# Attention masks as two products of 64 rows, and rope of k and square sums over both halves at once, in a six-layer windowed attention kernel

## The chip, the cores and the metric

The kernel runs on one core of a Trainium2 chip. The metric is device time in microseconds (us) of one execution. Five engines work side by side and meet through semaphores: TensorE (PE, matrix products and transposes; its weight loads are PEld), VectorE (DVE), ScalarE (ACT), GpSimd (POOL) and SyncE (SP, which issues the DMAs). SBUF is the working memory of 128 partitions, PSUM has 8 banks of 512 float32 a partition, into which TensorE writes.

## The reference, cut to what matters

The input `x` is (8, 512, 128). It is normalized, and the output is `x` plus a causal attention with relative positions plus a stack of six layers. Only the six layers matter here. Each has an attention over windows of 32 positions with 16 heads of 64, and then a gated feed-forward part:

```python
def attn_layer(x, Wqkv, qs, ksc, Wo):          # WINDOW = 32, HEADS = 16, DIM_HEAD = 64
    q, k, v = jnp.split(x @ Wqkv, 3, -1)       # each (b, n, 1024), then per head
    q = l2norm(q) * qs
    k = l2norm(k) * ksc
    q = q * cos * scale + rotate_half(q) * sin * scale
    k = k * cos * inv + rotate_half(k) * sin * inv
    out = local_attention(q, k, v)
    return out.reshape(b, n, INNER) @ Wo

def local_attention(q, k, v):                  # bk2, bv2: the window before and the own one
    mask = (it < jb) | (it > jb + w) | (jb == -1)
    sim = jnp.einsum('bhwie,bhwje->bhwij', bq, bk2) * QK_SCALE
    sim = jnp.where(mask, -jnp.finfo(sim.dtype).max, sim)
    attn = jax.nn.softmax(sim, -1)
    return jnp.einsum('bhwij,bhwje->bhwie', attn, bv2)

for i in range(DEPTH):                         # DEPTH = 6
    x = attn_layer(shift_tokens(x), Wqkv[i], q_scale[i], k_scale[i], Wo[i]) + x
    x = ffn_layer(shift_tokens(x), ln_g[i], ln_b[i], W1[i], b1[i], W2[i], b2[i]) + x
```

## The kernel before, in words

A first stage of about 570 us (`relative_attention`) computes the relative attention. Then `windowed_layers` runs the six layers, five in a hardware loop and the last written out. The order of work on every engine is written out by hand; semaphores with counts hold the engines together.

**Slots.** The attention of a layer goes over 8 sequences of 4 tiles with 128 positions each. A slot works on up to three tiles at a time: the new one ("age 0": project, square, rope), the one before ("age 1": turn q and k, masks, scores), and the one before that ("age 2": softmax, values, output product). `slot(lay, s, t, ages)` on each engine writes one slot. Of the 33 slots of a layer 32 have age 1, and 30 have both ages 0 and 2.

**TensorE in a slot** (L1370 to L1414): project v half 0 (bank 7), k halves 0 and 1 (banks 4 and 5) and q half 0 (bank 6), three products each of 128 by 512; turn the weights of half 0 (`turn_weights`, waits for `e_made` and `pw_made`); project q half 1 (bank 7); turn the weights of half 1; `mix_half(0)`, 64 small products of 64 rows by 32 columns; `turn_q(0)` and `turn_q(1)`, eight transposes into banks 4 and 5, which must wait until the rope of k has read those banks; `mix_half(1)`; project v half 1 into bank 6, which waits for the rope of q half 0; `turn_k(0)`, `turn_mixed(0)`, `turn_mixed(1)`, `turn_k(1)`; the masks; `score_half(0)`, 64 small products; the output product, 16 products (L1410); `score_half(1)`, which releases `s_mm`. The wait of `turn_q` is

```python
if project_new:
    pe.wait_ge(rk_made, at(T, 0, 2, c + 1))
```

**Masks** (L1402 to L1405): scores are made in banks 2 and 3, even heads (`par` 0) and odd heads (`par` 1). Before the scores each bank is filled with the mask, as a product of the identity (bfloat16, 128 by 128) with the mask of 128 rows, repeated for 8 heads to 512 columns; the scores are added onto it.

**VectorE in a slot** (L1776 to L1829): row maxima over both banks (L1782, waits for `s_mm`); two subtractions (L1788), each releasing `e_made`; rope of k half 0, half 1, rope of q half 0 (`rope_half`, three operations each: L1740 with 512 elements, L1741 and L1742 with 256); for each half of the mixed values a reciprocal and a product (`on`, L1810 and L1812); rope of q half 1; `lengths`: two sums of squares (L1747, 1024 elements each), then `square_root`, a chain of small operations that begins with L1755; at last the sum into `state` (L1826).

**ScalarE in a slot** does, in this order: copy v half 0, square k half 0 (L1562), exponentials half 0 (L1587, waits for `e_made`), square k half 1, exponentials half 1, copy turned weights half 0, square q half 0, and so on. `square` releases `sqk_made` or `sqq_made` by 1 per half, and waits for `ss_made` of the tile before.

**GpSimd in a slot** carries a part of kT (L1210), adds the two parts of the rope for k and for q (L1176, 1024 elements), refines the inverse square roots (L139 to L145) and scales q and k (L1181); in every second slot it splits half of the next input (L1057).

The `opening` of a layer, during the feed-forward part of the layer before, makes the first tile with `rope_half` and `lengths` in another order.

Of the kernel before, what the change touches and what calls it, by code (L numbers as in the profile page):

```python
# [25 lines left out]
X = mybir.AxisListType.X  # L26
# [26 lines left out]
C_FART = C_FAR + P  # L53
C_NEAR = C_FART + P
C_PART = C_NEAR + H
# [5 lines left out]
def constants():  # L61
# [20 lines left out]
    c[:, C_MQ:C_MQ + 2 * W] = shut  # L82
    first = (np.arange(P)[:, None] < W) & (k2 < W)
    c[:, C_MQ0:C_MQ0 + 2 * W] = np.where(first, MASKED, shut)
    far = np.where(np.arange(P)[None, :] >= np.arange(P)[:, None], MASKED, 0.0)
    c[:, C_FAR:C_FAR + P] = far
    c[:, C_FART:C_FART + P] = far.T
    c[0, C_NEAR:C_NEAR + H] = MASKED
# [12 lines left out]
def bc(ap, where, n):  # L101

    ap = ap.unsqueeze(where)
    return ap.broadcast_to([n if i == where else m for i, m in enumerate(ap.shape)])
# [768 lines left out]
def windowed_layers(nc, Wqkv, qs, ks, Wout, ln_g, ln_b, W1, b1, W2, b2, state, total, rank, out):  # L873
# [8 lines left out]
    with ExitStack() as ctx:  # L882
# [50 lines left out]
        ident = rank["const"][:, C_ID:C_ID + P]  # L933
        id_bf, mask_bf, mean_w = rank["id_bf"], rank["mask_bf"], rank["mean_w"]
        mask_q = {t: mask_bf[:, 2 * W * (t == 0):2 * W * (t == 0) + 2 * W] for t in range(TPS)}
# [73 lines left out]
        def at(T, back, n, i):  # L1009


            return n * (T - back + CREDIT) + i
# [234 lines left out]
        def _(pe):  # L1247
# [45 lines left out]
            def slot(lay, s, t, ages):  # L1293
# [106 lines left out]
                if score:  # L1400
                    turn_k(1)
                    pe.wait_ge(on_made, at(T, 2, 2, 2))  # L1402
                    for par in range(2):
                        pe.matmul(PS[:, 2 + par, :], id_bf[:], bc(mask_q[tile1], 1, PAIRS),
                                  start=True, stop=False, skip_group_check=True)  # L1405
                    score_half(0)
# [298 lines left out]
        def _(dve):  # L1705
# [25 lines left out]

            def rope_half(T, t, i, c, bank, squared, turned, added, done):
                dve.wait_ge(squared, at(T, 0, 2, c + 1))
                dve.wait_ge(turned, at(T, 2, 2, 2))
                dve.wait_ge(added, at(T, 1, 1, 1))
                src = PS[:, bank, :].rearrange("p (h d) -> p h d", h=8)
                cols = slice(512 * c, 512 * (c + 1))
                o1 = t1[:, t % 2, i, cols].rearrange("p (h d) -> p h d", h=8)
                o2 = t2[:, i, cols].rearrange("p (h d) -> p h d", h=8)
                dve.tensor_tensor(o1, src, bc(rope[:, 2 * i, t, :], 1, 8), ALU.mult)  # L1740
                dve.tensor_tensor(o2[:, :, 0:32], src[:, :, 32:64], bc(rope[:, 2 * i + 1, t, 0:32], 1, 8), ALU.mult)  # L1741
                dve.tensor_tensor(o2[:, :, 32:64], src[:, :, 0:32], bc(rope[:, 2 * i + 1, t, 32:64], 1, 8),  # L1742
                                  ALU.mult).then_inc(done, 1)

            def square_sum(T, i, squared):
                dve.wait_ge(squared, at(T, 0, 2, 2))
                dve.tensor_reduce(ss[:, H * i:H * (i + 1)], sq[:, i, :].rearrange("p (h d) -> p h d", h=H),  # L1747
                                  X, ALU.add).then_inc(ss_made, 1)

# [20 lines left out]
            def lengths(T):  # L1770
                square_sum(T, 0, sqq_made)
                square_sum(T, 1, sqk_made)
                square_root(T)

            def slot(lay, s, t, ages):
# [21 lines left out]
                if 0 in ages:  # L1797
                    rope_half(T, t, 1, 0, 4, sqk_made, kt_mm, addk_made, rk_made)
                    rope_half(T, t, 1, 1, 5, sqk_made, kt_mm, addk_made, rk_made)
                    rope_half(T, t, 0, 0, 6, sqq_made, qt_mm, addq_made, rq_made)  # L1800
# [150 lines left out]
```

## Time and profile before

| | us |
|---|---|
| median of 3 runs | 3954.24 (3954.11 to 3961.58) |
| the profiled execution, its own time | 3959.98 |
| its span in the profile | 3958.2 |
| TensorE busy | 3716.9 (94%) |
| VectorE busy | 3286.9 (83%) |
| GpSimd busy | 2598.7 (66%) |
| ScalarE busy | 2178.6 (55%) |

The span is the time from the first to the last instruction in the trace. Times of rows are measured from its start. An engine counts as busy while an instruction runs; TensorE's products overlap, and their ends are modelled, so the distance from one start to the next says more of their cost than their length. Idle time is put down to what ended it; "issue" is idle time in which no semaphore was waited for.

### The profile page before, as it was taken

Reading aid. Unit: us, or ns where it says so; the run is one execution under the profiler, and the core shown is the slowest. Engines: PE = TensorE matmul, PEld = TensorE weight load, DVE = VectorE, ACT = ScalarE, POOL = GpSimd, SP = SyncE. Lnnn points to the kernel's source line nnn. Section 1 sums busy time; section 2 is a strip of 40 time slices with the busy share of each in tenths; the row PEclk is TensorE's granted clock in tenths of the full one; section 3 lists DMA queues with packets and bytes.
Section 4 is the critical chain, followed back from the end, with each engine's and each line's share of the span. In section 5 each row is a group of like instructions: output and inputs, shape, how many; then the busy total and the mean of one; then the engine's idle time right before and its main releaser. Section 6 shows DMA issues by size and latency. Waiting matters only on the chain.

```text
span 3958.2 us, 165481 instructions
## 1 busy us (share of the span) xinstructions
PE 3716.9 (94%) x67712; PEld 2864.8 (72%) x67712; DVE 3286.9 (83%) x6981; ACT 2178.6 (55%) x3886; POOL 2598.7 (66%) x3029
## 2 busy tenths in 40 slices
PE   6999979999999999999999999999999999999998
PEld 3555547878767787677787677787677776777776
DVE  7666659999789899788998798997889897888886
ACT  3555545666546666456665465665466564565552
POOL 4555538887457777368787287874577773687770
PEclk8999989999999999999999999999999999999999
DMA  1000012222212222122222122222122221222220
GB/s 43 4 6 4 6 34 66 57 56 59 58 34 58 60 60 58 35 53 56 60 60 52 33 65 60 56 57 56 35 57 60 60 56 37 53 55 59 60 52 22
DMA packets 136325, 189.11 MB, mean 48 GB/s; under 512 B 38006, under 2 KB 58484, under 8 KB 135412
## 3 DMA queue, kind: packets, MB, share of 16 engines
q1 hardware_dynamic: 135540, 178.17, 17.6%
q8 instruction: 551, 9.03, 1.0%
q14 instruction: 234, 1.92, 0.2%
HBM read 22.61 MB, written 2.10 MB: 6 GB/s over the span
## 4 chain that ended last, share of the span: by engine, by line
POOL 39%; PE 22%; issue 20%; DVE 2%; POOLq 2%; ACT 0%; DMA 0%; SPq 0%; DVEq 0%; ACTq 0%
POOL t L1176 18%; POOL t L1181 8%; PE PS L1264 3%; PE PS L1250 3%; POOL xl L1057 3%; PE PS L1469 2%; PE PS L1252 2%; PE PS L1251 2%; POOL rn L145 2%; PE PS L1410 2%; POOL rn_tmp L141 2%; POOL rn_tmp L143 2%; POOL rn_tmp L139 2%; PE PS L1288 2%; PE PS L1274 1%
## 5 line engine op out<-in xcount | busy, mean ns | idle before, releaser
L1176 POOL TENSOR_TENSOR t<-t 128x1024 f32<-128x1024 f32 x384 | 908.3, 2373 | 263.3 <-DVE t L1742 263.3
L1535 ACT ACTIVATE va<-PS 128x512 f32<-128x512 f32 x384 | 230.1, 599 | 956.3 <-PE PS L1252 956.3
L1181 POOL TENSOR_TENSOR t<-t,rn 128x1024 f32<-128x1024 f32 x384 | 724.1, 1907 | 28.4 <-POOL rn L145 25.9
L1740 DVE TENSOR_TENSOR t<-PS,rope 128x512 f32<-128x512 f32 x768 | 521.7, 679 | 23.6 <-ACT sq L1562 18.1
L1250 PE MATMUL PS<-w_hi,xh 128*128 128x512 f32 x1152 | 514.8, 447 | 25.7 <-DVE xl L1057 10.1
L1562 ACT ACTIVATE sq<-PS 128x512 f32<-128x512 f32 x768 | 455.7, 594 | 38.3 <-PE PS L1252 22.3
L1252 PE MATMUL PS<-w_lo,xh 128*128 128x512 f32 x1152 | 460.8, 400 | 0.0
L1251 PE MATMUL PS<-w_hi,xl 128*128 128x512 f32 x1152 | 458.9, 398 | 0.0
L1264 PE MATMUL PS<-constants,t 128*128 128x128 f32 x3072 | 444.7, 278 | 9.5 <-POOL t L1181 7.6
L1747 DVE TENSOR_REDUCE ss<-sq 128x16 f32<-128x1024 f32 x384 | 448.0, 1207 | 0.0
L1264 PEld LDWEIGHTS PS<-constants,t 128*128 128x128 f32 x3072 | 352.8, 142 | 58.2 <-POOL t L1181 9.9
L1410 PE MATMUL PS<-oT,w_out 128*128 128x128 f32 x3072 | 393.3, 281 | 0.0
L1288 PE MATMUL PS<-vs,shared 64*32 64x65 f32 x18432 | 337.2, 225 | 45.3 <-issue 45.3
L1410 PEld LDWEIGHTS PS<-oT,w_out 128*128 128x128 f32 x3072 | 357.8, 191 | 17.7
L1274 PEld LDWEIGHTS PS<-kT,qT 64*32 64x32 f32 x24576 | 273.9, 105 | 127.3 <-issue 103.3
L1274 PE MATMUL PS<-kT,qT 64*32 64x64 f32 x24576 | 342.7, 225 | 15.0 <-POOL kT L1210 7.8
L1288 PE MATMUL PS<-va,shared 64*32 64x65 f32 x6144 | 338.9, 225 | 14.6 <-issue 14.6
L1288 PEld LDWEIGHTS PS<-vs,shared 64*32 64x32 f32 x18432 | 265.0, 105 | 111.0 <-issue 110.8
L1741 DVE TENSOR_TENSOR t<-PS,rope 128x256 f32<-128x256 f32 x768 | 316.3, 412 | 0.0
L1742 DVE TENSOR_TENSOR t<-PS,rope 128x256 f32<-128x256 f32 x768 | 315.8, 411 | 0.0
L1782 DVE TENSOR_REDUCE m<-PS 128x16 f32<-128x1024 f32 x192 | 234.9, 1224 | 87.4 <-PE PS L1274 85.2
L1250 PEld LDWEIGHTS PS<-w_hi,xh 128*128 128x128 f32 x1152 | 218.3, 190 | 95.7 <-issue 30.0
(172 smaller groups left out, 8112.8 us busy)
## 6 DMA issues: line engine op xcount, KB each, us to landing
vs<-va SPq DMA_DIRECT2D x768, 130.0 KB
vs<-va SPq DMA_DIRECT2D x768, 65.0 KB
t<-in_L_ffn_Wqkv SPq DMA_DIRECT2D x18, 512.0 KB, 4.4
w_out<-in_L_ffn_Wo SPq DMA_DIRECT2D x6, 512.0 KB, 3.9
a_normed<-in_L_attn_x SPq DMA_DIRECT2D x8, 256.0 KB, 6.4
a_xo<-in_L_attn_x SPq DMA_DIRECT2D x8, 256.0 KB, 2.9
out<-total SPq DMA_DIRECT2D x8, 256.0 KB, 3.5
w_raw<-in_L_ffn_W SPq DMA_DIRECT2D x6, 341.0 KB
```

Source lines behind the costliest of these rows:

```text
L1176: pool.tensor_tensor(mine[:, i, :], mine[:, i, :], t2[:, i, :], ALU.add).then_inc(done, 1)
L1181: pool.tensor_tensor(h, h, bc(rn[:, H * i:H * (i + 1)], 2, HB), ALU.mult).then_inc(done, 1)
L1250: pe.matmul(out, hi, w_hi, start=True, stop=False)
L1251: pe.matmul(out, lo, w_hi, start=False, stop=False)
L1252: return pe.matmul(out, hi, w_lo, start=False, stop=True)
L1264: last = pe.transpose(PS[:, bank, P * j:P * (j + 1)], source(j), ident)
L1274: last = pe.matmul(PS[W * w:W * (w + 1), 2 + par, 2 * W * pair:2 * W * (pair + 1)], qT[rows, pair, W * w:W * (w + 1)], kT[rows, t % 2, pai ...
L1288: last = pe.matmul(PS[W * w:W * (w + 1), (0, 2)[c] + par, HB1 * (pair % 4):HB1 * (pair % 4 + 1)], pT[rows, pair, W * w:W * (w + 1)], v, st ...
L1410: last = pe.matmul(PS[:, y_at, 0:P], w_out[:, pair, :], oT[:, pair, :], start=(pair == 0), stop=(pair == PAIRS - 1))
L1562: act.activation(sq[:, i, 512 * c:512 * (c + 1)], PS[:, bank, :], ACT.Square).then_inc(done, 1)
L1740: dve.tensor_tensor(o1, src, bc(rope[:, 2 * i, t, :], 1, 8), ALU.mult)
L1747: dve.tensor_reduce(ss[:, H * i:H * (i + 1)], sq[:, i, :].rearrange("p (h d) -> p h d", h=H), X, ALU.add).then_inc(ss_made, 1)
```

## The change

Three edits. The masks are no longer made with the identity and 128 rows. A new constant table of 128 columns (`C_SEL`, two copies over 64 rows each) picks for each of the 128 queries its row among 64, so that rows 0 to 63 of the mask are enough for bank 2 and rows 64 to 127 for bank 3. The table comes as bfloat16 with the masks, as part of `mask_bf`. The rope of k is one call over 16 heads in place of two calls over 8; it waits for both squares, reads banks 4 and 5 together, and releases `rk_made` by 2 at its end. The two square sums are one operation over 2048 elements, which releases `ss_made` by 2. The rope of q and the openings keep the halves.

```diff
+C_SEL = C_FART + P
+C_NEAR = C_SEL + P
...
-    first = (np.arange(P)[:, None] < W) & (k2 < W)
+    first = (np.arange(P)[:, None] % (2 * W) < W) & (k2 < W)
...
+    row, query = np.arange(P)[:, None] % (2 * W), np.arange(P)[None, :]
+    c[:, C_SEL:C_SEL + P] = np.where(query < W, query == row, query % W + W == row)
...
-        id_bf, mask_bf, mean_w = rank["id_bf"], rank["mask_bf"], rank["mean_w"]
+        mask_bf, mean_w = rank["mask_bf"], rank["mean_w"]
+        sel_bf = mask_bf[:, C_SEL - C_MQ:C_SEL - C_MQ + P]
...
                     for par in range(2):
-                        pe.matmul(PS[:, 2 + par, :], id_bf[:], bc(mask_q[tile1], 1, PAIRS),
+                        rows = slice(HB * par, HB * (par + 1))
+                        pe.matmul(PS[:, 2 + par, :], sel_bf[rows, :], bc(mask_q[tile1][rows, :], 1, PAIRS),
                                   start=True, stop=False, skip_group_check=True)
...
-            def rope_half(T, t, i, c, bank, squared, turned, added, done):
-                dve.wait_ge(squared, at(T, 0, 2, c + 1))
+            def rope_heads(T, t, i, heads, src, squared, turned, added, done):
+                n = heads.stop - heads.start
+                dve.wait_ge(squared, at(T, 0, 2, heads.stop // 8))
                 dve.wait_ge(turned, at(T, 2, 2, 2))
                 dve.wait_ge(added, at(T, 1, 1, 1))
-                src = PS[:, bank, :].rearrange("p (h d) -> p h d", h=8)
-                cols = slice(512 * c, 512 * (c + 1))
-                o1 = t1[:, t % 2, i, cols].rearrange("p (h d) -> p h d", h=8)
-                o2 = t2[:, i, cols].rearrange("p (h d) -> p h d", h=8)
-                dve.tensor_tensor(o1, src, bc(rope[:, 2 * i, t, :], 1, 8), ALU.mult)
-                dve.tensor_tensor(o2[:, :, 0:32], src[:, :, 32:64], bc(rope[:, 2 * i + 1, t, 0:32], 1, 8), ALU.mult)
-                dve.tensor_tensor(o2[:, :, 32:64], src[:, :, 0:32], bc(rope[:, 2 * i + 1, t, 32:64], 1, 8),
-                                  ALU.mult).then_inc(done, 1)
...
-            def square_sum(T, i, squared):
-                dve.wait_ge(squared, at(T, 0, 2, 2))
-                dve.tensor_reduce(ss[:, H * i:H * (i + 1)], sq[:, i, :].rearrange("p (h d) -> p h d", h=H),
-                                  X, ALU.add).then_inc(ss_made, 1)
+                src = src.rearrange("p (h d) -> p h d", h=n)
+                o1 = t1[:, t % 2, i, :].rearrange("p (h d) -> p h d", h=H)[:, heads, :]
+                o2 = t2[:, i, :].rearrange("p (h d) -> p h d", h=H)[:, heads, :]
+                dve.tensor_tensor(o1, src, bc(rope[:, 2 * i, t, :], 1, n), ALU.mult)
+                dve.tensor_tensor(o2[:, :, 0:32], src[:, :, 32:64], bc(rope[:, 2 * i + 1, t, 0:32], 1, n), ALU.mult)
+                dve.tensor_tensor(o2[:, :, 32:64], src[:, :, 0:32], bc(rope[:, 2 * i + 1, t, 32:64], 1, n),
+                                  ALU.mult).then_inc(done, n // 8)
+
+            def rope_half(T, t, i, c, bank, squared, turned, added, done):
+                rope_heads(T, t, i, slice(8 * c, 8 * (c + 1)), PS[:, bank, :], squared, turned, added, done)
...
             def lengths(T):
-                square_sum(T, 0, sqq_made)
-                square_sum(T, 1, sqk_made)
+                dve.wait_ge(sqq_made, at(T, 0, 2, 2))
+                dve.wait_ge(sqk_made, at(T, 0, 2, 2))
+                dve.tensor_reduce(ss[:], sq[:].rearrange("p i (h d) -> p (i h) d", h=H), X, ALU.add).then_inc(ss_made, 2)
                 square_root(T)
...
-                    rope_half(T, t, 1, 0, 4, sqk_made, kt_mm, addk_made, rk_made)
-                    rope_half(T, t, 1, 1, 5, sqk_made, kt_mm, addk_made, rk_made)
+                    rope_heads(T, t, 1, slice(0, H), PS[:, 4:6, :].rearrange("p b n -> p (b n)"),
+                               sqk_made, kt_mm, addk_made, rk_made)
                     rope_half(T, t, 0, 0, 6, sqq_made, qt_mm, addq_made, rq_made)
```

## Rows read from the trace of the kernel before

Columns of a timeline: start in us from the start of the span, length in us, engine, line, operation, output<-inputs, array form (rows*columns for TensorE), shape, type, count merged; in brackets the idle time before and what ended it.

**Rows 1.** Busy time by engine in 500 us inside the layers; clock, DMA.

```profile
2000.00:2500.00 500.00, 476.60 (x9395) 378.10 (x9374) 431.77 (x934) 281.29 (x522) 341.57 (x408) 0.99 0.21 53
```

**Rows 2.** Waits: who waited for whom, us in total, times, longest.

```profile
PEld PS L1274 <- issue: 103.3, 229, 3.1
...
DVE m L1782 <- PE PS L1274: 85.2, 156, 1.2
...
PE PS L1288 <- issue: 59.9, 76, 1.5
```

**Rows 3.** Timeline of TensorE in one slot: start, length, line.

```profile
2020.13 1.09 PE L1264 MATMUL PS<-constants,t 128*128 128x128 f32 x8
...
2021.94 0.50 PE L1250 MATMUL PS<-w_hi,xh 128*128 128x512 f32 x1
...
2024.49 0.59 PE L1404 MATMUL PS<-mask_bf,id_bf 128*128 128x512 bf16 x2
```

**Rows 4.** Timeline of VectorE in the same slot.

```profile
2017.24 0.68 DVE L1740 TENSOR_TENSOR t<-PS,rope 128x512 f32<-128x512 f32 x1
2017.84 0.41 DVE L1741 TENSOR_TENSOR t<-PS,rope 128x256 f32<-128x256 f32 x1
2018.17 0.41 DVE L1742 TENSOR_TENSOR t<-PS,rope 128x256 f32<-128x256 f32 x1
...
2019.43 0.41 DVE L1742 TENSOR_TENSOR t<-PS,rope 128x256 f32<-128x256 f32 x1
2019.76 0.68 DVE L1740 TENSOR_TENSOR t<-PS,rope 128x512 f32<-128x512 f32 x1
...
2023.83 0.41 DVE L1742 TENSOR_TENSOR t<-PS,rope 128x256 f32<-128x256 f32 x1
2024.16 2.33 DVE L1747 TENSOR_REDUCE ss<-sq 128x16 f32<-128x1024 f32 x2
...
2028.68 1.23 DVE L1782 TENSOR_REDUCE m<-PS 128x16 f32<-128x1024 f32 x1 [0.41 <-PE PS L1274]
```

**Rows 5.** Timeline of ScalarE, this slot and the one before.

```profile
2003.34 0.58 ACT L1562 ACTIVATE sq<-PS 128x512 f32<-128x512 f32 x1
...
2016.87 0.62 ACT L1587 ACTIVATE shared<-shared 128x512 f32<-128x512 f32 x1
2017.39 0.59 ACT L1562 ACTIVATE sq<-PS 128x512 f32<-128x512 f32 x1
```

**Rows 6.** Timeline of TensorE, turn of q in the slot before.

```profile
2006.07 1.09 PE L1264 MATMUL PS<-constants,t 128*128 128x128 f32 x8
```

**Rows 7.** Timeline of GpSimd's adds and of VectorE's L1755.

```profile
2008.56 4.70 POOL L1176 TENSOR_TENSOR t<-t 128x1024 f32<-128x1024 f32 x2
...
2024.32 2.37 POOL L1176 TENSOR_TENSOR t<-t 128x1024 f32<-128x1024 f32 x1 [0.56 <-DVE t L1742]
...
2012.47 0.84 DVE L1755 TENSOR_SCALAR ss<-ss 128x32 f32<-128x32 f32 x1
```

**Rows 8.** Timeline of TensorE in narrow windows, at changes of form.

```profile
2010.33 0.27 PE L1264 MATMUL PS<-constants,t 128*128 128x128 f32 x1
2010.43 0.59 PE L1404 MATMUL PS<-mask_bf,id_bf 128*128 128x512 bf16 x2
...
2010.65 0.38 PE L1404 MATMUL PS<-mask_bf,id_bf 128*128 128x512 bf16 x1
2010.96 0.27 PE L1274 MATMUL PS<-kT,qT 64*32 64x64 f32 x6
...
2005.07 0.27 PE L1264 MATMUL PS<-constants,shared 128*128 128x128 f32 x1
2005.28 0.24 PE L1288 MATMUL PS<-vs,shared 64*32 64x65 f32 x1
```

**Rows 9.** Groups by line: busy, mean ns, idle before.

```profile
L1274 PE MATMUL PS<-kT,qT 64*32 64x64 f32 x24576 | 342.7, 225 | 15.0 <-POOL kT L1210 7.8 <-issue 5.7
```

**Rows 10.** Timeline of GpSimd at the start of the run.

```profile
16.75 0.61 POOL L381 COPY state<-a_xT 128x513 f32<-128x513 f32 x1 [4.08 <-ACT a_xT L660]
```

More of the change, by code:

```diff
@@ L53 @@
 C_FART = C_FAR + P
-C_NEAR = C_FART + P
+C_SEL = C_FART + P
+C_NEAR = C_SEL + P
 C_PART = C_NEAR + H
```

## Prediction

> **What bounds the kernel.** I read the busy times by stretches first. In 500 us of the windowed layers TensorE is busy 476.6 us and VectorE 431.8, at a granted clock of 0.99 [rows 1]. So the clock is at its upper level (2.4 GHz) and two engines are near full. To decide between them I read one slot of the layers on each engine's timeline. The masks of one tile start at 2010.43 and of the next at 2024.49, so a slot takes 14.06 us [rows 3, 8]. In it TensorE goes from one group to the next with no wait for another engine that is worth naming: turn of q, second half of the mixed values, projection, turns, masks, scores, output product, scores. VectorE is done earlier: before it takes the row maxima it sits idle 0.41 us for the last score [rows 4], and over the run that wait comes 156 times, 85.2 us in all [rows 2]. Hence a delay of TensorE shows in full in the time, and VectorE has about half a microsecond of room in a slot. There is one more loss on TensorE: 59.9 us in 76 pauses "for issue" inside the products of weights and values, where no semaphore is waited for [rows 2]. A delay just ahead of such a pause may be swallowed by it.
>
> **Part 1, the rope of k over both halves.** It replaces six operations by three. Spacing on VectorE is 0.60 us for 512 elements a partition (2017.24 to 2017.84) and 0.33 for 256 (2017.84 to 2018.17) [rows 4], that is about 0.06 fixed and 0.27 for 256 elements. With 1024, 512 and 512 elements the three take 1.14 + 0.60 + 0.60 = 2.34 in place of 6 operations with 2.52 (2017.24 to 2019.76). The work shrinks by 0.18 us a slot.
>
> But the new first operation needs the squares of *both* halves, since it waits for sqk at heads.stop // 8 = 2, where the first half of the old form waited for 1. ScalarE makes them in its own order: square of half 0, exponentials of half 0 (which wait for VectorE's subtraction), square of half 1. In this slot the exponentials start at 2016.87 and the second square runs 2017.39 to 2017.98 [rows 5]. VectorE comes free at 2017.24. It must now wait until about 2018.03 (0.05 for the handover; the nearest row is 0.08 from VectorE's end at 2024.24 to GpSimd's start at 2024.32 [rows 4, 7]). All that is queued behind on VectorE starts later: the rope of q, reciprocals, on, the square sums.
>
> Who waits for it: the rope's result is now released once, at its end. 2018.03 + 1.14 + 0.60 + 0.68 (the last 512 end to end) = 2020.45, against 2019.84 for the second half now. TensorE's turn of q writes banks 4 and 5, from which the rope reads, and waits for this; it starts at 2020.13 now [rows 3]. With 0.05 of handover it starts at 2020.50, a stall of 0.35 to 0.37. The slot before says the same: second square ends 2003.92 [rows 5], plus 0.05 + 2.42 + 0.05 = 2006.44, and the turn of q started at 2006.07 [rows 6]: 0.37. I take 0.35, a little lower because the handovers may be 0.03. The bounds: 0.25, if the longer operations have a smaller fixed part than I take, and 0.45.
>
> What comes after has room. The rope of q's first half would end at 2018.03 + 2.34 + 0.60 + 0.33 + 0.41 = 2021.71; the projection that waits for it starts at 2021.94 now and at 2022.29 after the stall [rows 3]. The second result of on trails TensorE's own products, so it moves by the same 0.35 and no more. So the stall is paid once per slot. It comes in slots that have both a new tile and weights to turn: 30 in each of 6 layers, 180. Gross 180 x 0.35 = 63 us.
>
> How much of it falls into the pauses for issue? They stand right behind the turn of q, in the second half of the mixed values. 76 pauses of 0.79 us mean [rows 2] could take at most 76 x 0.35 = 27 us. I take 22, since some are shorter than the stall. Net +41 us; bounds +18 (0.25 x 180 = 45, less 27) and +81 (0.45, none swallowed).
>
> **Part 2, square sums at once.** The two reductions take 2.33 us [rows 4] and become one; by the fixed part that saves 0.06. I cost it at nothing, because the next operation, the maximum with 1e-24 in L1755, doesn't start freely. In the slot where GpSimd's two adds run from 2008.56 for 4.70 us, to 2013.26, this small operation begins at 2012.47 and lasts 0.84, to 2013.31 [rows 7]. It ends with the add. In the other slot the add of q starts 0.08 behind the rope and takes 2.37 [rows 7], as long as the reductions. Saving at most 192 x 0.06 = 12 us of VectorE time, it is covered by GpSimd's add and then by VectorE's 0.41 of idle time; the bound is 0 to 2 us of gain, for slots without that idle time.
>
> **Part 3, masks on 64 rows each.** Per slot two products of 128 rows and 512 columns become two of 64 rows in different halves of the array and different banks. Do such halves run together? The score products (64 rows by 32 columns, alternating halves) take 342.7 us for 24576, 14 ns each though one lasts 225 [rows 9]; so many run at once, in both halves. So the second mask should start next to the first, saving the 0.22 between 2010.43 and 2010.65 [rows 8]. What speaks against it is the change of form. From the last turn to the first mask, both 128 by 128, it is 0.10 (2010.33 to 2010.43), but from the last turn to products of 64 by 32 it is 0.21 (2005.07 to 2005.28) [rows 8]. And from the second mask to the scores it is 0.31 (2010.65 to 2010.96), 0.09 more than mask to mask. Each change of form costs 0.09 to 0.11. Now there is one between turns and scores; then there are two, 128x128 to 64x128 to 64x32. From last turn to first score: now 0.10 + 0.22 + 0.31 = 0.63; after 0.21 + 0.01 + 0.31 = 0.53. Gain 0.10 to 0.12 by rounding; 0.11 x 192 tiles = 21 us. Bounds: 0.22 x 192 = 42 if the step to 64x128 is free, and a loss of 0.11 x 192 = 21 if the halves run one behind the other.
>
> The Trainium skill has both sides: TensorE: Matmul & The Clock Gate (Part 3, measured speedup) has tiles in different row groups start about 4 ns apart, with no price for the change, which makes 42; TensorEngine Tiling (Array Packing), Key Properties, says that changing the mode drains the array, which makes 21. Rows 8 agree with the second.
>
> Not all of it is kept. The loads of the score products wait for issue 103.3 us in 229 pauses, nearly all hidden behind products [rows 2], but the second half of the scores, after the output product, is sometimes held up by them; with masks that end earlier such pauses grow. I take a third away: gain 14 us.
>
> The new table of 128 columns makes one load and one cast at the start longer. GpSimd, which casts, is idle 4.08 us right after that work until ScalarE releases it [rows 10], and the cast is well under that: nothing.
>
> **The sum.** 41 - 14 - 0 = +27 us. The profiled execution took 3959.98 with a span of 3958.2; its layers' slots are those of every run. Against the median of 3954.2 this gives 3981. A change under 0.2%, 8 us, can't be told from none here.
>
> **Rivals.**
> 1. *The change of form is free* (chance 0.12). Gain 42 less a third = 28; 3954 + 41 - 28 = 3967. For: the halves surely run together in the scores. Against: [rows 8].
> 2. *Issue swallows the stall in all slots* (0.13), the case on the other side. TensorE would be paced by how its instructions arrive, and a pause lets them get ahead, so that later pauses vanish too: 59.9 us of them [rows 2] would pay for the 63. Then 3954 + 3 - 21 = 3936. It becomes "faster" only where less than 13 of the 63 us are left beside the full 21 of the masks. Against: the pauses stand in 76 of 192 slots, and the slot shown runs without any. The Trainium skill (Runtime: NRT & Kernel Launch, Instruction fetch mechanics) has instructions arrive in blocks of 256; no row here shows a block's arrival.
> 3. *Nothing is swallowed* (0.12): 3954 + 63 - 14 = 4003, if the pauses only move behind the stall.
> 4. *Halves one behind the other* (0.05): 3954 + 41 + 21 = 4016, or a little less where pauses hide part.
> 5. *The change does nothing that shows* (0.10): VectorE's wait of 0.8 us is there, but stall and masks cancel, the stall nearer to 0.25. 45 - 27 = 18, less 14 to 21: 3954, from 3946 to 3962.
> My forecast has 0.48.
>
> **Numbers.** 3981, range 3950 to 4004: it leaves out rival 2, rival 4 and an edge of rival 5, together 0.2. The forecast's own range is 3970 to 3998. Faster: rival 2, 0.13. Same: rival 5 and the low edge of rival 1, 0.12. Slower 0.75.
>
> **What the profile after would show.** The first rope operation with 1024 elements with an idle of 0.7 to 0.9 us before it, released by ScalarE's square, about 180 times. The turn of q idle before it 0.35, released by VectorE's rope. Masks with 64 rows, a few ns apart, 0.2 behind the last turn. Pauses for issue in the mixed values smaller by about 20 us. The idle before the row maxima still above 0.2. I am wrong if the turn of q doesn't wait, if the pauses shrink by much more than 27 us, or if the two masks lie 0.2 apart.

## The result and the profile after

The changed kernel takes 3996.03 us in the median of 4 runs (3992.15 to 3999.37), the kernel before beside it 3954.3 us: a ratio of 1.0095, 95% interval 1.0076 to 1.0115. That is 42 us slower by the medians, 38 by the ratio. The forecast was +27, that is 3981, with a range of 3950 to 4004. The profiled execution of the changed kernel has a span of 3997.3 us, 39 more than before.

The waits of the changed kernel (who waited for whom, us in total, times, longest):

```profile
DVE t L1749 <- ACT sq L1569: 153.4, 192, 3.2
...
DVE m L1790 <- PE PS L1280: 94.0, 174, 1.1
...
PE PS L1270 <- DVE t L1751: 76.2, 182, 2.0
...
PE PS L1294 <- issue: 33.7, 69, 1.1
```

Two waits have grown from little. VectorE's first rope operation (now L1749) waits for ScalarE's square 153.4 us in 192 places, where the kernel before has 18.1 us in 14. TensorE's transposes (now L1270) wait for VectorE's rope 76.2 us in 182 places, where it has 1.3 us. One line shrank: the pauses for issue in the mixed values, 59.9 us before, are 33.7. VectorE's idle time before the row maxima, 94.0 us in all, is larger than the 85.2 of [rows 2], so VectorE isn't what holds the next slot back.

One slot of the changed kernel, first ScalarE, then VectorE, then TensorE (timeline: start, length, engine, line, ..., idle time before):

```profile
2022.10 0.63 ACT L1594 ACTIVATE shared<-shared 128x512 f32<-128x512 f32 x1
2022.63 0.58 ACT L1569 ACTIVATE sq<-PS 128x512 f32<-128x512 f32 x1
```

```profile
2023.24 1.23 DVE L1749 TENSOR_TENSOR t<-PS,rope 128x1024 f32<-128x1024 f32 x1 [0.81 <-ACT sq L1569]
2024.39 0.68 DVE L1750 TENSOR_TENSOR t<-PS,rope 128x512 f32<-128x512 f32 x1
2024.98 0.68 DVE L1751 TENSOR_TENSOR t<-PS,rope 128x512 f32<-128x512 f32 x1
2025.58 0.68 DVE L1749 TENSOR_TENSOR t<-PS,rope 128x512 f32<-128x512 f32 x1
```

```profile
2025.81 1.06 PE L1270 MATMUL PS<-constants,t 128*128 128x128 f32 x8 [0.38 <-DVE t L1751]
```

It reads like [rows 4] and [rows 5] with the wait put in. On ScalarE the exponentials of half 0 come first, and the second square ends at 2023.21. The rope starts 0.03 later, after 0.81 us idle. Its three operations take 1.15, 0.59 and 0.68 us, the first two counted to the next start. TensorE turns q 0.15 us after the last of them ends (2025.66).

The masks, in a narrow window of TensorE's timeline, and where the scores begin:

```profile
2015.18 0.27 PE L1270 MATMUL PS<-constants,t 128*128 128x128 f32 x1
2015.38 0.39 PE L1411 MATMUL PS<-mask_bf 64*128 64x512 bf16 x2
...
2015.70 0.28 PE L1280 MATMUL PS<-kT,qT 64*32 64x64 f32 x7
```

Both masks lie within 0.39 us, one mask's length, and start 3 ns apart in the median (in [rows 8] two took 0.59). The first starts 0.20 behind the last turn, where it was 0.10, and the scores start 0.32 behind the masks. From last turn to first score it is 0.52 in place of 0.63: a gain of 0.11, as the sum had it.

### The profile page after: what moved, and what is told of

Read it like the earlier page. It is cut to its first block, busy times and chain, and to the rows that moved or that the text cites. A ratio compares the mean times of both kernels' runs of the same rounds, so it can differ in the third digit from the quotient of the medians.

```text
span 3997.3 us, 164737 instructions
## 1 busy us (share of the span) xinstructions
PE 3708.9 (93%) x67712; PEld 2857.6 (71%) x67712; DVE 3235.6 (81%) x6231; ACT 2176.8 (54%) x3886; POOL 2597.8 (65%) x3029
## 4 chain that ended last, share of the span: by engine, by line
POOL 31%; PE 26%; issue 19%; DVE 5%; ACT 2%; POOLq 1%; DMA 0%; DVEq 0%; SPq 0%; ACTq 0%
POOL t L1182 15%; POOL t L1187 6%; PE PS L1270 5%; PE PS L1417 3%; PE PS L1280 3%; PE PS L1256 3%; PE PS L1476 3%; PE PS L1258 2%; PE PS L1257 2%; POOL xl L1063 2%; POOL rn L150 2%; POOL rn_tmp L146 2%; POOL rn_tmp L148 2%; PE PS L1294 2%; POOL rn_tmp L144 2%
## 5 line engine op out<-in xcount | busy, mean ns | idle before, releaser
L1749 DVE TENSOR_TENSOR t<-PS,rope 128x512 f32<-128x512 f32 (+1 forms) x582 | 496.8, 854 | 158.3 <-ACT sq L1569 153.4
L1270 PE MATMUL PS<-constants,t 128*128 128x128 f32 x3072 | 440.1, 277 | 81.7 <-DVE t L1751 76.2
L1270 PEld LDWEIGHTS PS<-constants,t 128*128 128x128 f32 x3072 | 355.2, 142 | 135.1 <-issue 103.0
L1780 DVE TENSOR_REDUCE ss<-sq 128x32 f32<-128x2048 f32 x192 | 436.4, 2273 | 0.0
L1417 PEld LDWEIGHTS PS<-oT,w_out 128*128 128x128 f32 x3072 | 358.0, 191 | 18.1 <-issue 0.3
L1542 ACT ACTIVATE qT<-PS 128x512 f32<-128x512 f32 x384 | 208.8, 595 | 149.4 <-PE PS L1270 149.2
L1750 DVE TENSOR_TENSOR t<-PS,rope 128x256 f32<-128x256 f32 (+1 forms) x582 | 289.8, 498 | 0.0
L1751 DVE TENSOR_TENSOR t<-PS,rope 128x256 f32<-128x256 f32 (+1 forms) x582 | 289.4, 497 | 0.0
```

Of the source, the lines that this page charges most:

```text
L1270: last = pe.transpose(PS[:, bank, P * j:P * (j + 1)], source(j), ident)
L1417: last = pe.matmul(PS[:, y_at, 0:P], w_out[:, pair, :], oT[:, pair, :], start=(pair == 0), stop=(pair == PAIRS - 1))
L1542: copy = lambda o, i: act.activation(o, i, ACT.Copy)
L1749: dve.tensor_tensor(o1, src, bc(rope[:, 2 * i, t, :], 1, n), ALU.mult)
```

## The experiments

Each experiment was timed beside the kernel before, in four groups. That kernel's own median was 3962.7, 3964.4, 3965.9 and 3978.7 us in them, against 3954.3 beside the changed kernel, so the ratios are what is compared.

### Each part alone

**masks_only**, the changed kernel with the rope of k and the square sums as before:

```diff
-                    rope_heads(T, t, 1, slice(0, H), PS[:, 4:6, :].rearrange("p b n -> p (b n)"),
-                               sqk_made, kt_mm, addk_made, rk_made)
+                    rope_half(T, t, 1, 0, 4, sqk_made, kt_mm, addk_made, rk_made)
+                    rope_half(T, t, 1, 1, 5, sqk_made, kt_mm, addk_made, rk_made)
...
-                dve.tensor_reduce(ss[:], sq[:].rearrange("p i (h d) -> p (i h) d", h=H), X, ALU.add).then_inc(ss_made, 2)
+                for i, squared in enumerate((sqq_made, sqk_made)):
+                    dve.wait_ge(squared, at(T, 0, 2, 2))
+                    dve.tensor_reduce(ss[:, H * i:H * (i + 1)], sq[:, i, :].rearrange("p (h d) -> p h d", h=H),
+                                      X, ALU.add).then_inc(ss_made, 1)
```

> The kernel before with the masks on 64 rows alone (rope of k and square sums as before). My theory: from the last turn to the first score TensorE needs 0.11 us less in each of 192 tiles, 21 us, of which issue pauses in the second half of the scores take back a few: 3954 - 17 = 3937, ratio 0.995 to 0.997, with no waits of the turn of q for VectorE's rope. Rival, the extra change of form costs more than the pairing gains and the masks are part of the loss: 3960 or more. Rival, the change of form only shows in these few starts and the gain is the full 0.21: 3918 to 3925.

Measured: ratio 0.996 (0.9944 to 0.9975), 16 us faster. The masks are the good part, of the size of the sum's net term (14). TensorE's transposes wait for the rope only 3.1 us, in 6 places.

**rope_only**, the kernel before with only `rope_heads` and its call for k (the call is shown):

```diff
-                    rope_half(T, t, 1, 0, 4, sqk_made, kt_mm, addk_made, rk_made)
-                    rope_half(T, t, 1, 1, 5, sqk_made, kt_mm, addk_made, rk_made)
+                    rope_heads(T, t, 1, slice(0, H), PS[:, 4:6, :].rearrange("p b n -> p (b n)"),
+                               sqk_made, kt_mm, addk_made, rk_made)
```

> The kernel before with the rope of k over both halves alone. My theory: the whole loss is here. The turn of q waits 0.40 to 0.45 us for VectorE in 180 slots, 72 to 80 us, of which 25 to 30 fall into pauses for issue: 3954 + 50 = 4004, range 3998 to 4012, ratio 1.011 to 1.015, more than the full change. Rival, the loss comes from another part (the single square sum, the masks): this one stays within 3950 to 3975. Rival, the loss of the full change needs both, because the masks' saved time makes the stall longer: 3975 to 3990.

Measured: ratio 1.0104 (1.0085 to 1.0124), 41 us slower. Its waits:

```profile
DVE t L1742 <- ACT sq L1562: 152.8, 192, 4.5
...
PE PS L1264 <- DVE t L1744: 76.0, 182, 2.0
...
PE PS L1288 <- issue: 36.3, 72, 1.1
```

These are the three lines of the changed kernel again, within 3 us, without the masks. So the loss is here, and the stall doesn't depend on the masks. The time came 9 us below the 50 that I expected.

**sums_only**, the kernel before with the single square sum of the change:

```diff
-                square_sum(T, 0, sqq_made)
-                square_sum(T, 1, sqk_made)
+                dve.wait_ge(sqq_made, at(T, 0, 2, 2))
+                dve.wait_ge(sqk_made, at(T, 0, 2, 2))
+                dve.tensor_reduce(ss[:], sq[:].rearrange("p i (h d) -> p (i h) d", h=H), X, ALU.add).then_inc(ss_made, 2)
```

> The kernel before with the two square sums as one operation. My theory: 0.06 us less of VectorE work per slot, hidden by GpSimd's add that the next small operation waits for and by VectorE's idle time before the row maxima: 3952 to 3956, ratio 0.999 to 1.001. Rival, VectorE is on the path in many slots: 192 x 0.06 = 12 us faster, 3942. Rival, the later release of the first half's sum holds up ScalarE's square of the next k: slower by more than 4 us.

Measured: ratio 1.0005 (0.9993 to 1.0018), no difference. Where the saved 0.06 us went shows in the operation behind the sum:

```profile
L1755 DVE TENSOR_SCALAR ss<-ss 128x32 f32<-128x32 f32 x192 | 84.4, 440 | 6.6
```

It lasts 440 ns in the mean; before, its 192 took 75.2 us, 392 ns each, so 9 of the 12 us are lost again here. In 182 of the 192 places it starts while GpSimd's add runs, and there it always ends 0.03 to 0.04 us after the add does (worked out from the trace).

**masks_sums**, the changed kernel with only the rope of k back in halves (the first part of the diff of masks_only).

> The changed kernel with the rope of k back in two halves: masks on 64 rows and one square sum. My theory: the two good parts without the bad one, 3934 to 3940, ratio 0.995 to 0.997, the same as the masks alone within 3 us. Rival, the parts interact (the shorter masks bring VectorE onto the path, so that the shorter sum now counts): 3925 to 3932, clearly below the masks alone.

Measured: ratio 0.9977 (0.9957 to 0.9997), just above the range expected. It isn't told apart from the masks alone; there is no sign that the shorter sum counts.

### What in the rope costs: the wait or the width

**first_in_halves**, the changed kernel, but the first rope operation of k in two halves, each behind its own square:

```diff
-                dve.wait_ge(squared, at(T, 0, 2, heads.stop // 8))
+                if n < H:
+                    dve.wait_ge(squared, at(T, 0, 2, heads.stop // 8))
...
-                dve.tensor_tensor(o1, src, bc(rope[:, 2 * i, t, :], 1, n), ALU.mult)
+                if n == H:
+                    for c in range(2):
+                        part = slice(8 * c, 8 * (c + 1))
+                        dve.wait_ge(squared, at(T, 0, 2, c + 1))
+                        dve.tensor_tensor(o1[:, part, :], src[:, part, :], bc(rope[:, 2 * i, t, :], 1, 8), ALU.mult)
+                else:
+                    dve.tensor_tensor(o1, src, bc(rope[:, 2 * i, t, :], 1, n), ALU.mult)
```

> The changed kernel, but the first of the three rope operations of k is made in two halves, each waiting for its own square; the other two stay over both halves. My theory: the cost is the wait for ScalarE's second square ahead of the first operation, not the width. VectorE then works through half 0 while the second square is made, the rope ends 0.5 us earlier, 0.1 ahead of the turn of q, and the stall of 0.44 is gone: ratio to before 0.995 to 0.998, as masks_sums. Rival, the single release of both halves at the end is what costs: the turn of q still waits more than 0.2 us in most slots, ratio 1.004 or more.

Measured: ratio 0.9963 (0.9949 to 0.9977). VectorE in one slot, and TensorE's wait for the rope over the whole run:

```profile
2000.36 0.68 DVE L1754 TENSOR_TENSOR t<-PS,rope 128x512 f32<-128x512 f32 x1
2001.25 0.69 DVE L1754 TENSOR_TENSOR t<-PS,rope 128x512 f32<-128x512 f32 x1 [0.21 <-ACT sq L1569]
2001.86 0.68 DVE L1757 TENSOR_TENSOR t<-PS,rope 128x512 f32<-128x512 f32 x1
2002.46 0.68 DVE L1758 TENSOR_TENSOR t<-PS,rope 128x512 f32<-128x512 f32 x1
```

```profile
PE PS L1270 <- DVE t L1758: 5.8, 4, 1.8
```

Half 0 is worked on while the second square is made. In the slot shown 0.21 us of idle time are left, where the slot of the changed kernel had 0.81, and the turn of q waits in 4 places in place of 182. The release is still single and two operations still span both halves. So the cost is the wait ahead of the first operation. This version is faster than both kernels (15 us under the kernel before), as masks_only is, and has four rope operations for k in place of six. Against six (masks_sums, 0.9977) the gain of having four isn't told from none.

**after_mix_first**, the changed kernel with other work put over the late rope:

```diff
+                if mix:
+                    mix_half(1)
                 if score:
                     turn_q(0)
                     turn_q(1)
-                if mix:
-                    mix_half(1)
```

> The changed kernel with TensorE's second half of the mixed values ahead of the turn of q, so that 0.8 us of other work lies over the late rope. My theory: no wait of the turn of q for VectorE is left (0 in place of 76 us). But two halves of 64 small products then stand back to back; if pauses for issue end at a moment that is set by how fast instructions arrive, they grow by up to the 1.0 us of the turn that no longer stands ahead of them in some 70 slots, and take the gain back: ratio to before 1.000 to 1.008. Rival, pauses don't depend on what stands ahead: the 0.44 is regained in all slots, ratio 0.990 to 0.997.

Measured: ratio 1.0117 (1.0099 to 1.0135), slower than I expected, and no better than the change. The wait of the transposes for the rope is no longer among TensorE's longest waits, but the pauses for issue are back, and larger:

```profile
PE PS L1294 <- issue: 98.1, 77, 2.4
```

98.1 us against 33.7 in the changed kernel and 59.9 in the kernel before, in about as many places (77, 69, 76). With the turn of q no longer between them, the two bursts of 64 small products take in the mean 2.31 us from start to start over 174 slots, where twice the undisturbed 0.79 would be 1.58 (worked out from the starts in the trace). So a pause in the second burst grows when the work between the bursts is taken away, and shrinks when a stall is put there. That is why the stall of the change was partly swallowed. The wait for the rope is gone (7.4 us in 4 places) but the time isn't, so it isn't enough to move the cover.

The pauses are not the whole of it. TensorE's granted clock was 0.970 to 0.977 in these six runs, against 0.980 to 0.982 in the changed kernel's four. One of the stretches behind it, a pause and then the clock (the windows view: stretch, length, busy time of PE, PEld, DVE, ACT and POOL, granted clock, DMA):

```profile
2112.93 0.24 PE L1294 MATMUL PS<-va,shared 64*32 64x65 f32 x1 [2.01 <-issue]
2114.40:2117.60 3.20, 3.20 (x14) 2.81 (x13) 3.20 (x5) 2.05 (x5) 1.84 (x1) 0.50 0.03 8
```

In this trace 15 stretches of 3.4 us at the lower level of the clock (1.2 GHz) lie in the middle of a layer's attention. Each begins during a pause for issue of 1.6 to 2.4 us in the mixed values or at most 1.4 us after it. 24 other pauses longer than 1.5 us have none behind them. The changed kernel, whose longest such pause is 1.1 us, has no such stretch. Behind the first stage (from 580 us on) the clock is at the lower level for 145 us in all, against 93 in the changed kernel. Taken as half speed for the difference of 52 us, that is up to 26 us (an estimate), more than the 14 us between the two profiled executions. The median period of a slot is 14.21 us against 14.63 in the changed kernel. So the move did gain the stall in the usual slot, and the long pauses lost it again together with the clock.

**after_act_order**, the changed kernel with ScalarE's second square first:

```diff
-                if 2 in ages:
-                    weigh(0)
                 if 0 in ages:
                     square(T, 1, 1, 5, k_mm, sqk_made)
+                if 2 in ages:
+                    weigh(0)
```

> The changed kernel with ScalarE's square of k half 1 ahead of the exponentials of half 0. My theory: VectorE's wait ahead of the rope of k falls from 0.8 to about 0.55 us, but the exponentials come 0.7 us later, TensorE waits some 0.6 us ahead of the first turn of the weights and no longer at the turn of q: ratio to before 1.011 to 1.020, slower than the change. Rival, the exponentials have room on TensorE's side: the stall only shrinks to 0.2 us and the ratio falls to 1.000 to 1.006.

Measured: ratio 1.0286 (1.0266 to 1.0306), 2.9% slower than the kernel before and worse than the range I gave (to 1.020). The place was right and the size too small:

```profile
PE PS L1270 <- ACT shared L1594: 148.5, 192, 4.7
...
PE PS L1294 <- issue: 63.7, 78, 2.4
```

TensorE now waits 148.5 us for the exponentials (28.1 in the kernel before), 0.77 in the mean, and its wait for the rope ahead of the turn of q is down to 6.8 us. The pauses in the mixed values are back at 63.7. The stall of 0.77 us stands ahead of the first turn of the weights, before both bursts, and they swallow nothing of it; only a stall between the bursts was swallowed. The exponentials have no room on TensorE's side, so this order on ScalarE is no way out.

### The price of a change of form, and of instructions

**masks_small**, masks_sums with the masks in the form of the scores:

```diff
+                    pe.sem_inc(s_begun, 1)
+                    for w in range(NW):
                         for par in range(2):
                             rows = slice(HB * par, HB * (par + 1))
-                            pe.matmul(PS[:, 2 + par, :], sel_bf[rows, :], bc(mask_q[tile1][rows, :], 1, PAIRS),
+                            pe.matmul(PS[W * w:W * (w + 1), 2 + par, :], sel_bf[rows, W * w:W * (w + 1)],
+                                      bc(mask_q[tile1][rows, :], 1, PAIRS),
                                       start=True, stop=False, skip_group_check=True)
```

> masks_sums (rope of k in halves) with the masks in eight products of 64 rows by 32 columns, the form of the scores, in place of two of 64 by 128; a semaphore is raised once more ahead of them. My theory: one change of form less between turns and scores. From the last turn to the first score 0.21 + 0.22 = 0.43 us in place of 0.53: 192 x 0.10 = 19 us less than masks_sums, part of it lost to issue pauses, ratio to before 0.991 to 0.995. Rival, the eight products don't all run together or their loads take the time: the same as masks_sums or slower, 0.997 or more.

Measured: ratio 1.0035 (1.0021 to 1.0049), slower than the kernel before and than masks_sums. The masks themselves did as expected:

```profile
2010.24 0.27 PE L1270 MATMUL PS<-constants,t 128*128 128x128 f32 x1
2010.44 0.41 PE L1413 MATMUL PS<-mask_bf 64*32 64x512 bf16 x8
2010.66 0.84 PE L1280 MATMUL PS<-kT,qT 64*32 64x64 f32 x64
```

From last turn to first score it is 0.42 us, 0.10 less than with two of 64 by 128. So one change of form less is worth 0.10 here. But a pause for issue of 5 us stands in the mixed values near the end of the first layer, and again in each of the four other looped layers, beginning at 1632, 2199, 2765 and 3329 us; the last layer, written out, has none:

```profile
1066.85 0.26 PE L1294 MATMUL PS<-va,shared 64*32 64x65 f32 x1 [5.11 <-issue]
1066.10:1072.70 6.60, 5.85 (x30) 4.65 (x30) 1.56 (x3) 1.38 (x3) 0.00 (x0) 0.50 0.01 2
```

The second row (the windows view again) shows that the pause costs more than its length: within its last 2.1 us, in all five places, a stretch of 6.8 us begins in which the granted clock is at its lower level. From the last masks of a looped layer to the first of the next it takes 108 to 109 us, where masks_sums has 99 to 103: 39 us more in the five, of which 25 are the pauses. The clock is at its lower level there for 55 us, and for 21 in masks_sums. Within the attention of the layers this kernel is 8 us faster than masks_sums (2743 against 2752 us, worked out from the starts of the masks). So the form of the scores does pay, but the pause takes several times as much.

**before_pad**, the kernel before with four more increments a slot, 128 a layer, on TensorE's queue:

```diff
+                if score:
+                    for _ in range(4):
+                        pe.sem_inc(s_begun, 1)
                 if project_new:
```

> The kernel before with four more semaphore increments per slot on TensorE's queue, ahead of the projections, where TensorE has long products; no other work changes. It shifts where blocks of instructions begin. My theory: the pauses for issue in the small products hang on the count of instructions ahead of them, so their number and size change (their total in the mixed values moves away from 60 us by more than 5, up or down) and the time moves with them by 0.1 to 0.5 per cent. Rival, the pauses come from the work itself or from the transfers: same total within 5 us and ratio 0.999 to 1.001.

Measured: ratio 1.0257 (1.0239 to 1.0274). Both expectations missed: the increments themselves cost. TensorE's pauses for issue ahead of the projection are 79.9 us in 186 places, 8.2 in 10 before:

```profile
PE PS L1250 <- issue: 79.9, 186, 2.3
```

In 174 slots the time from the second half of the scores to the next projection rose from 0.91 to 1.36 us in the mean (from the starts in the trace), 0.11 for each increment. The pauses in the mixed values kept their total (59.4 in 82), so these regular pauses were not shown to hang on the count. But a new pause of about 4 us (3.6 to 4.2) appeared once in each looped layer, in the projections of the feed-forward part:

```profile
1083.39 0.59 PE L1252 MATMUL PS<-fl,w_hi 128*128 128x512 f32 x1 [4.16 <-issue]
```

**masks_small_pad**, masks_small with three more increments a slot, at the place that before_pad has them, 96 a layer.

> masks_small with three more semaphore increments per slot, 96 a layer, so that each layer holds 512 instructions more than in masks_sums. My theory: the pause of 5 us for issue that masks_small has once in each of five looped layers, in the mixed values of the last slot, is set by where a block begins and goes away: 25 to 40 us less than masks_small, ratio to before 0.991 to 0.997. Rival, that pause comes from the eight small mask products themselves: it stays, ratio 1.002 or more.

Measured: ratio 1.0095 (1.0079 to 1.0111). The pause of 5 us is gone (the longest in the mixed values is 1.9 us, 66.8 us in 85), as my theory had it. From the last masks of a looped layer to the first of the next the five take 36 us less than in masks_small, within the 25 to 40 that I gave. But the ratio isn't what I said, since the increments cost about as much each as in before_pad: the attention of the layers takes 56 us more.

**small_pad_halves**, masks_small_pad with the rope of first_in_halves.

> masks_small_pad with the rope of k as in first_in_halves (first operation in halves, the other two over both). The best version if the pause goes away: ratio to before 0.990 to 0.996, within 0.002 of masks_small_pad, since VectorE isn't what sets the time. Rival, with the masks shorter VectorE is now on the path and its shorter rope counts: 0.003 below masks_small_pad or more.

Measured: ratio 1.0098 (1.0081 to 1.0116), the same as masks_small_pad, and outside the range expected for the same reason. VectorE's shorter rope isn't worth anything here either.

**small_halves**, first_in_halves with the eight small masks and no increment more (the scores' own stands ahead of the masks, with the waits of the first scores):

```diff
+                    pe.wait_ge(carried, at(T, 1, 1, 1))
+                    pe.wait_ge(qT_made, at(T, 1, 2, 1))
+                    pe.wait_ge(kT_made, at(T, 1, 2, 1))
+                    pe.sem_inc(s_begun, 1)
+                    for w in range(NW):
                         for par in range(2):
...
-                    score_half(0)
+                    score_pairs(tile1, range(4))
```

> first_in_halves with the masks in eight products of 64 rows by 32 columns, now with no semaphore increment more than before (the one ahead of the scores stands ahead of the masks). 384 instructions a layer more than first_in_halves, 32 fewer than masks_small. My theory: 0.1 us less from turns to scores in 192 tiles, 19 us, and the pause of 5 us for issue near the end of each looped layer is gone or not according to the count of instructions: without it ratio to before 0.990 to 0.995, with it 0.997 to 1.001. Rival, part of what masks_small lost was the increment at 0.1 us a slot: then the period of a slot falls by another 0.1 us against masks_small.

Measured: ratio 1.0067 (1.0045 to 1.0089), worse than either expectation. The long pause is there again, at another place, once in each looped layer:

```profile
1076.79 0.80 PE L1258 MATMUL PS<-fl,w_hi 128*128 128x512 f32 x1 [4.16 <-issue]
```

and the pauses in the small products grew as well (74.2 us in 87 in the mixed values, against 55.2 in 71 in first_in_halves). The rival fell too: inside a layer a slot takes 14.54 us in the mean, in place of 14.42 in masks_small. Since the waits of the scores now stand ahead of the masks and the rope differs, that isn't the price of the increment alone.

## Why the prediction was right

By its own steps:

**The bound.** TensorE was the path, as read. masks_only takes about 21 us of TensorE's work away and the time falls by 16; shorter work on VectorE (sums_only, small_pad_halves) moved nothing. One thing was not weighed: the profile's page puts 39% of the chain that ended last in the kernel before on GpSimd and 22% on TensorE. But from the first masks on TensorE is idle for GpSimd for only 20 us in all, against 74 for issue, so GpSimd isn't what sets the time of a slot.

**The wait of the rope for the second square.** Shown: 0.81 us in the slot above, 153.4 us over the run. first_in_halves shows that it is this wait and not the width that costs.

**The stall at the turn of q.** Shown, and the term that was mis-sized. I took 0.35 x 180 = 63 us; the trace has 76.2 us in 182 places. In 178 of them the mean is 0.38, 68 us together, 5 more than I took. The other 8 us are four waits of 2.0 us, in the first slot with a turn of four looped layers, which I had left out. In the kernel before the transposes and the projection waited there too (0.43, 0.46 and 0.60 us in one such slot), so it isn't all loss. The stall of the ordinary slot is near the forecast partly by luck: the rope's length was right to 0.01 us, but the handover from VectorE to the transposes takes 0.15 us in every one of the 182 places, where I put 0.05. Taken alone that would have made the stall 0.45. Part of the other way is the handover from ScalarE, 0.03 in place of 0.05; for the rest the runs don't say.

**What the pauses swallow.** 22 us taken, 59.9 - 33.7 = 26 seen, 59.9 - 36.3 = 24 in rope_only. Of the 59.9 us 57.5 stand in the burst right behind the turn of q, as I had it, and of the 33.7 it is 29.9. after_mix_first shows it from the other side: with no work between the bursts the pauses are 98 us. Rival 2, pauses that swallow everything, fell: they come in only some 70 places, and a stall in the other slots is paid. Rival 3, nothing swallowed, had 4003, and by the time alone it lies nearer to the measured 3996 than my 3981 does. The trace decides against it, since the pauses did shrink by 26 us.

**The square sums.** Nothing, as costed, and for the reason given.

**The masks.** Gross 0.11 us a slot, as read from the starts, to the hundredth. Net 14 us taken, 16 measured (10 to 22). The third that I took away isn't shown: the pauses of the score products' loads shrank, from 103.3 to 67.9 us in masks_only, where I said that they grow, and TensorE's pauses ahead of the scores grew only from 5.7 to 8.2 us. Rival 1 (no price for the form) and rival 4 (one behind the other) fell by the trace: the halves run together and the change of form costs 0.10. Of the two rules of the Trainium skill that I set against each other, the drain at a change of mode (TensorEngine Tiling (Array Packing), Key Properties) is what the trace agrees with: 0.20 us from the last turn to the first mask, where it was 0.11. The start about 4 ns apart (TensorE: Matmul & The Clock Gate, Part 3, measured speedup) holds as well, 3 ns here, but doesn't include the change.

**The sum.** With the sizes seen: 76 - 26 - 16 = 34, against 38 by the ratio and 27 forecast. Rival 5, stall and masks cancel, fell with the stall of 0.38. The measured 3996 lies at the upper edge of the forecast's own range (3970 to 3998). The parts timed alone multiply to 1.0104 x 0.996 = 1.0064, and the whole change gave 1.0095. The intervals just about allow for that (1.0104 has 0.002 to each side, 0.996 has 0.0016, 1.0095 has 0.002). By the medians themselves the gap is 7 us in place of 12 (4004.6 - 15.3 = 3989.3 against 3996.0), since the kernel before was 8 us faster beside the changed kernel than beside the parts. A term that I hadn't in the sum is the clock: from 580 us on the profiled execution of the changed kernel is at the lower level for 93 us, that of the kernel before for 74, by half speed at most 10 us (an estimate). But masks_only has 87 and is faster, so it isn't shown that the change brings this. What the last 4 to 12 us are stays open.

## What to carry to other kernels

When two operations are merged, ask first what each waited for: the merged one starts at the later of the two and releases at the end, and 0.18 us of saved work bought 0.8 us of waiting, of which 0.4 reached the engine that sets the time. If they are to be merged, merge the operations that come after the wait and keep the first one split: here that removed the loss, and gained nothing that could be told from six operations. Cost an array change by the distance between starts at the edges of the group, not only by the products inside it. And when a kernel of the same work is slower, compare the granted clock before explaining all of it by waits.

## What the runs showed of the hardware

- A single semaphore increment on TensorE's queue, ahead of a projection, cost 0.11 us each (before_pad, 4 of them: 0.45 us a slot, +2.6% over the run together with the new pause).
- Once in each pass of the loop over layers TensorE may pause for issue for 3.6 to 5.1 us. It was there with 128, 384 and 416 instructions a layer more than in the kernels without it, in the mixed values or in the feed-forward projections, and absent with 0 and 512 more; the layer outside the loop never had it. A period of 256 instructions fits these counts and so does one of 512; no run had 256 more.
- Behind each of these 15 pauses (masks_small, before_pad, small_halves), at most 2.1 us before or after its end, a stretch of 3.4 to 6.8 us begins in which the granted clock is at its lower level.
- Eight products of 64 by 32 with 512 columns ran together: 0.41 us for all, where one of 128 by 128 takes 0.38.
- A handover from VectorE or ScalarE to TensorE's transposes that wait for it takes 0.14 to 0.15 us, from end to start, in every place measured (182 in the changed kernel, 192 in after_act_order).
- A pause for issue in the second of two bursts of small products depends on what stands between them: nothing there makes it longer (98 us), a stall there makes it shorter (34 us, against 60), a stall ahead of both leaves it (64 us).
